# Small layernorm steps moved from VectorE to GpSimd, with new orders on all engines, in a four-layer graph network on one core

## The reference

```
h = relu(layernorm(x));  x = x + deg*(h Wi + b) + adj (h Wj)                    # layer 0
h = relu(layernorm(x));  x = x + softmax(mask(leaky(src_i + dst_j))) (h W)      # layer 1, 0 for a row without neighbours
h = relu(layernorm(x));  x = x + [softmax(mask(leaky(src_i + dst_j))) g | g], g = h W   # layer 2
h = relu(layernorm(x));  x = x + multi-head attention(h), 8 heads of 32, masked # layer 3
layernorm(x) = (x - mean) / sqrt(variance + 1e-5)
```

## Time and profile before

| | |
|---|---|
| median of 3 runs | 1277.61 us |
| the profiled execution's own time | 1276.93 us |
| its span | 1275.1 us |
| TensorE busy | 1232.8 us (97%) |
| TensorE weight loads busy | 1134.8 us (89%) |
| VectorE busy | 1141.8 us (90%) |
| ScalarE busy | 1058.2 us (83%) |
| GpSimd busy | 944.5 us (74%) |
| granted TensorE clock, mean | 0.995 |

### The profile page before, as it was taken

How to read it: one execution, slowest core, us unless ns; L and a number is a source line. 1 busy time by engine, 2 the same in 40 slices (tenths; PEclk the granted TensorE clock), 3 DMA queues, 4 the chain that set the end, 5 groups by cost and what they waited for, 6 DMA issues and landing times. The chain is left out here.

```text
span 1275.1 us, 43341 instructions
## 1 busy us (share of the span) xinstructions
PE 1232.8 (97%) x12213; PEld 1134.8 (89%) x12213; DVE 1141.8 (90%) x5713; ACT 1058.2 (83%) x3911; POOL 944.5 (74%) x1338
## 2 busy tenths in 40 slices
PE   5799999999999999999999999999999999999997
PEld 4689999999999999999999998999999999999986
DVE  4689999989999999999999999999999999998874
ACT  2468898888888888888889888888889888888886
POOL 4568877877777877777787787777787777787663
PEclk9899999999999999999999999999999999999999
DMA  4011222222112122222112122222122122211001
GB/s 119 24 22 21 38 44 50 37 44 51 36 44 52 36 44 52 36 43 52 38 40 52 40 45 46 41 39 52 40 47 43 41 46 44 43 39 31 18 19 34
DMA packets 70586, 53.57 MB, mean 42 GB/s; under 512 B 20688, under 2 KB 70352, under 8 KB 70352
## 3 DMA queue, kind: packets, MB, share of 16 engines
q1 hardware_dynamic: 68144, 49.35, 19.2%
q10 hardware_dynamic: 2208, 1.45, 0.4%
HBM read 33.89 MB, written 16.89 MB: 40 GB/s over the span
## 5 line engine op out<-in xcount | busy, mean ns | idle before, releaser
L775 ACT ACTIVATE exps<-masked,nmax 128x128 f32<-128x128 f32 x1024 | 397.1, 394 | 0.0
L348 POOL TENSOR_TENSOR probs<-exps,rsum 128x512 f32<-128x512 f32 x256 | 266.7, 1042 | 162.6 <-DVE rsum L567 161.9
L319 POOL TENSOR_SCALAR y<-x,nm,rstd 128x256 f32<-128x256 f32 x512 | 282.8, 563 | 22.5 <-issue 21.0
L311 POOL TENSOR_TENSOR rstd<-veps,power 128x2 f32<-128x2 f32 x256 | 178.2, 696 | 114.4 <-DVE veps L472 109.3
L559 DVE CUSTOM_DVE_ANT_0 masked<-bank,mask 128x128 f32<-128x128 f32 x1024 | 232.0, 280 | 1.3 <-PE bank L986 0.8
L775 ACT ACTIVATION_READ_ACCUMULATOR exps<-masked,nmax 128x1 f32 x1024 | 198.4, 194 | 0.0
L876 PE MATMUL bank<-w_hi,ht_hi 128*128 128x512 f32 (+1 forms) x512 | 192.6, 376 | 4.5 <-DVE ht_lo L501 4.5
L456 DVE BATCH_NORM_STATS2 stats<-x 128x6 f32<-128x256 f32 x512 | 183.9, 411 | 0.2
L886 PE MATMUL bank<-ident,y 128*128 128x128 f32 x1024 | 159.0, 278 | 20.0 <-POOL y L319 19.3
L877 PE MATMUL bank<-w_lo,ht_hi 128*128 128x512 f32 (+1 forms) x512 | 175.4, 343 | 0.0
L878 PE MATMUL bank<-w_hi,ht_lo 128*128 128x512 f32 (+1 forms) x512 | 174.8, 341 | 0.0
(11 more groups left out here) (120 smaller groups left out, 3693.4 us busy)
## 6 DMA issues: line engine op xcount, KB each, us to landing
x<-in_x SPq DMA_DIRECT2D x64, 256.0 KB, 4.6
out<-x SPq DMA_DIRECT2D x64, 256.0 KB, 4.7
db<-rows SPq DMA_DIRECT2D x110, 128.0 KB, 4.1
rows<-dst SPq DMA_DIRECT2D x110, 1.0 KB, 3.0
probs<-in_w0t SPq DMA_DIRECT2D x1, 512.0 KB, 7.9
probs<-in_w1t ACTq DMA_DIRECT2D x1, 256.0 KB, 5.9
exps<-in_wot SPq DMA_DIRECT2D x1, 256.0 KB, 7.6
w_sb<-in_w ACTq DMA_DIRECT2D x1, 256.0 KB, 7.8
```

What stands on the lines that cost most here:

```text
L311: pool.tensor_tensor(rstd[i][:, b], veps[i][:, b], power[:], ALU.pow).then_inc(S[f"rstd{i}"], 1)
L319: last = pool.tensor_scalar(y[i][:, b, g], src[:, bx, g], nm[i][:, s, g:g + 1], rstd[i][:, s, g:g + 1], ALU.add, ALU.mult)
L348: pool.tensor_tensor(probs3[:, p % BUFFERS["probs3"], j], exps3[:, p % BUFFERS["exps3"], j], rsum3[:, s, j].unsqueeze(2).to_broadcast([P, ...
L775: last = act.activation(exps3[:, b, j, i], masked3[:, p % BUFFERS["masked3"], j, i], ACT.Exp, bias=nmax3[:, s, j, i:i + 1], scale=-1.0, ac ...
```

## The change

The eps addition and the negated mean of all four layernorms, and layer 1's product with the row flag, go from VectorE to GpSimd. `negative_mean` becomes an operation of its own with the names `nm0` to `nm3` and its own place in the list. `rstd` and `y` keep their instructions. `LAG`, `BANKS` and the order in every `step`, SyncE's too, are new; `BUFFERS` and `SMALL` are as before.

```diff
@@ GpSimd gains
+            def shifted_variance(i, p):
+                b = p % SMALL
+                passed(pool, f"mv{i}", p)
+                passed(pool, f"rstd{i}", p, SMALL)
+                pool.tensor_scalar(veps[i][:, b], mv[i][:, b, :, 1], LN_EPS, None, ALU.add).then_inc(S[f"veps{i}"], 1)
+
+            def negative_mean(i, reader, p):
+                b = p % SMALL
+                passed(pool, f"mv{i}", p)
+                passed(pool, reader, p, SMALL)
+                pool.tensor_scalar(nm[i][:, b], mv[i][:, b, :, 0], -1.0, None, ALU.mult).then_inc(S[f"nm{i}"], 1)
+
+            def clear_empty_rows(p):
+                s = p % SMALL
+                passed(pool, "rsum1_any", p)
+                pool.tensor_tensor(rsum[1][:, s], rsum[1][:, s], has_any[:].to_broadcast([P, G]), ALU.mult).then_inc(S["rsum1"], 1)
@@ VectorE loses
-            def shifted_variance(i, p):
-                b = p % SMALL
-                passed(dve, f"mv{i}", p)
-                passed(dve, f"y{i}", p, SMALL)
-                dve.tensor_scalar(veps[i][:, b], mv[i][:, b, :, 1], LN_EPS, None, ALU.add).then_inc(S[f"veps{i}"], 1)
-                dve.tensor_scalar(nm[i][:, b], mv[i][:, b, :, 0], -1.0, None, ALU.mult).then_inc(S[f"nm{i}"], 1)
-            def clear_empty_rows(p):
-                s = p % SMALL
-                passed(dve, "rsum1_any", p)
-                dve.tensor_tensor(rsum[1][:, s], rsum[1][:, s], has_any[:].to_broadcast([P, G]), ALU.mult).then_inc(S["rsum1"], 1)
@@ LAG, one line of 16 on either side
-       "row_in1": 0, "load": -4, "row_out2": 1, "store": 7, "row_out1": -1, "row_in2": 1, "e1t": 2, "h0t": -1, "pt0": 6, "wh0_mm": 1, "v_mm": 5,
+       "store": 8, "row_out1": 0, "row_in1": 0, "row_out2": 1, "load": -5, "row_in2": 1, "x2_mm": 2, "pt1": 6, "s0": 0, "wh0_mm": 1, "m1": -1,
```

More of the change, by code:

```diff
@@ L59 @@
[L59 to L72, removed]
@@ L73 @@
-    "x3b": (0, "x3_mm", ('x3',)),
-    "wh1": (2, "wh1_mm", ('wh1',)),
-    "hh": (1, "hh_mm", ('hh',)),
+    "x2b": (4, "x2_mm", ('x2',)),
+    "pt1": (2, "pt1", ('p3t_1',)),
+    "x1b": (5, "s0", ('x1',)),
+    "wh0": (0, "wh0_mm", ('wh0',)),
+    "m1": (4, "m1", ('mj_lo1', 't0_1')),
+    "h3t": (6, "h3t", ('h3t_lo',)),
+    "pt0": (3, "pt0", ('p3t_0',)),
+    "d2": (2, "d2", ('z2',)),
+    "pt3": (0, "pt3", ('p3t_3',)),
+    "x4b": (1, "x4_mm", ('x4',)),
+    "prep": (2, "products", ('w1_split',)),
@@ new lines @@
+    "m0": (5, "m0", ('mj_lo0', 't0_0')),
+    "qt": (6, "qt_mm", ('qt',)),
+    "h2t": (3, "h2t", ('ht2',)),
+    "at2": (2, "e2t", ('at2',)),
+    "kt": (4, "kt_mm", ('kt',)),
+    "d1": (3, "d1", ('z1',)),
+    "x3b": (1, "x3_mm", ('x3',)),
+    "h1t": (0, "h1t", ('h1t_lo',)),
+    "ot": (6, "ot_mm", ('ot_lo',)),
+    "sc0": (2, "scores", ('nmax3_0',)),
+    "sc1": (3, "scores", ('nmax3_1',)),
+    "sc2": (4, "scores", ('nmax3_2',)),
+    "sc3": (5, "scores", ('nmax3_3',)),
+    "hh": (1, "hh_mm", ('hh',)),
@@ L76 @@
+    "v": (0, "v_mm", ('v',)),
+    "h0t": (3, "h0t", ('h0t_lo',)),
+    "pt2": (1, "pt2", ('p3t_2',)),
+    "at1": (2, "e1t", ('at1',)),
+    "wh1": (6, "wh1_mm", ('wh1',)),
+    "prepa": (0, "adj_spread", ('adj_rows',)),
+    "zz1": (7, "z1", ('nmax1',)),
     "zz2": (7, "z2", ('nmax2',)),
[L77 removed]
 }
@@ L186, in gnn_kernel @@
         x_out = [sem(f"x_out{i}") for i in range(BUFFERS["x4"])]
-        S = {name: sem(name) for name in LAG if name not in ("row_in1", "load", "row_out2", "store", "row_out1", "row_in2")}
-        for name in ("nm0", "nm1", "nm2", "nm3",):
-            S[name] = sem(name)
+        S = {name: sem(name) for name in LAG if name not in ("store", "row_out1", "row_in1", "row_out2", "load", "row_in2")}
         def due(t, operation):
@@ L270, in step @@
                     write_row(1, t - LAG["row_out1"])
+                if due(t, "row_in1") and not at_an_end(t - LAG["row_in1"]):
+                    spread_row(1, t - LAG["row_in1"])
+                if due(t, "row_out2") and not at_an_end(t - LAG["row_out2"]):
+                    write_row(2, t - LAG["row_out2"])
+                if due(t, "load") and t - LAG["load"] >= 2:
+                    load(t - LAG["load"])
                 if due(t, "row_in2") and not at_an_end(t - LAG["row_in2"]):
@@ L585, in step @@
             def step(t):
+                if due(t, "stats0"):
+                    stats_of(0, x0, t - LAG["stats0"])
+                if due(t, "x4"):
+                    sum_x4(t - LAG["x4"])
                 if due(t, "rsum3_0"):
                     inverse_sum3(0, t - LAG["rsum3_0"])
+                if t == LAG["w0_low"]:
+                    low_w0()
+                if due(t, "qt"):
+                    add_bias("qt", qt, bq_sb, float(DH) ** -0.5, t - LAG["qt"])
+                if t == LAG["w1_split"]:
+                    split_w1()
@@ L588, in step @@
                 if due(t, "rsum2"):
                     inverse_sum(2, "rsum2", "x3", t - LAG["rsum2"])
+                if due(t, "mj_lo0"):
+                    low_mj(0, t - LAG["mj_lo0"])
+                if due(t, "t0_0"):
+                    add_own(0, t - LAG["t0_0"])
+                if due(t, "mv0"):
+                    mean_and_variance(0, t - LAG["mv0"])
+                if due(t, "kt"):
+                    add_bias("kt", kt, bk_sb, 1.0, t - LAG["kt"])
+                if due(t, "x3"):
+                    sum_x3(t - LAG["x3"])
@@ new lines, in step @@
+                if due(t, "exp3_1"):
+                    exps3_of(1, t - LAG["exp3_1"])
+                if due(t, "at1"):
+                    copy_exp_transposed(1, t - LAG["at1"])
+                if due(t, "h0t_hi"):
+                    relu_transposed_high(0, ht0_r, last_of("m0", "m1"), t - LAG["h0t_hi"])
+                if due(t, "v"):
+                    copy_v(t - LAG["v"])
+                if due(t, "wh1"):
+                    copy_projection1(1, t - LAG["wh1"])
+                if due(t, "p3t_2"):
+                    copy_p3_transposed(2, t - LAG["p3t_2"])
@@ new lines, in step @@
+                if due(t, "h3t_hi"):
+                    relu_transposed_high(3, ht3_r, last_of("kt_mm", "qt_mm", "v_mm"), t - LAG["h3t_hi"])
+                if due(t, "p3t_0"):
+                    copy_p3_transposed(0, t - LAG["p3t_0"])
+                if due(t, "z2"):
+                    sum_logits(2, hh, "hh", F1, t - LAG["z2"])
+                if due(t, "exp3_0"):
+                    exps3_of(0, t - LAG["exp3_0"])
+                if t == LAG["w3_high"]:
+                    round_w3()
```

313 lines of the change are left out of this document (130 added, 183 removed), and 21 rows, old and new, of the table LAG.

## The result

| | before | changed |
|---|---|---|
| median beside each other | 1277.3 us (1275.94 to 1278.38, 4 runs) | 1265.3 us (1264.62 to 1268.02, 4 runs) |
| span of the profiled execution | 1275.1 us | 1263.1 us |

That holds on this chip.

What follows compares the result with a forecast made beforehand. TensorE, busy 97%, was taken as the bound, with an 18.88 us pass. Disturbed passes -3.2, start +0.7 and the other ends +0.6 gave -1.9 us: median 1277.6 to 1275.7 us, own range 1272 to 1279, whole range 1267 to 1286.

Steps and rivals of the forecast that it cites:

- net of the filling and draining without the start: +0.6: Both ends besides the start: longer hops and new list places net to +0.6 us, bounds -8 and +6.
- signs of being wrong: Filling: among them, s0 (an aggregation's first matmul) of pass 8 starting more than 5 us away from 141.7.
- Filling, the hops: Layernorm chains: a hop to GpSimd adds +0.25 us to five y waits and one in the draining, +1.5.
- Filling, the lists: Filling, new order: scores behind kt_mm -1.2 us; layernorm 2 ahead of layernorm 1 on GpSimd -1.3 and +1.6.
- Draining: End of the run: ScalarE's work and the last pass's tail stay the same, 0 beyond one longer y chain.
- Start: First pass: r0 precedes the first veps on GpSimd, first transpose at 13.2 us, +0.7, bounds 0 and +1.3.
- GpSimd's cover: Steady pass: GpSimd needs 17.3 us of 18.88 with the added work, 1.6 us to spare, so no cost.
- Rival C: GpSimd becomes the bound: small instructions at 696 ns, pass 21.9 us, 1446 us in all; chance 0.03.
- VectorE: Steady pass: VectorE loses 2.18 us of 17.64, 15.46 remain; directly worth nothing.
- Disturbed passes: Steady part: half of the 6.5 us lost in disturbed passes goes, -3.2 us, bounds -6.5 and +8.
- rival B: Layernorm 1: mv1 behind nmax2 lets late rows reach y1 and h1t; 1292 us, or 1286; chance 0.15.
- Rival A: Ends: qt waits go, -2.4 us, filling's y waits halve, -3; with disturbed passes 1269.5 us; chance 0.17.

Runs made afterwards that it cites:

- e1_move: Kernel before with only the small instructions moved to GpSimd, lists and banks as before: 1302.63 us, ratio 1.0145.
- e7_thrice: Changed kernel with two more instructions of veps's form ahead of each veps on GpSimd, into an unread tile: 1281.64 us, ratio 1.0045.
- e9_h1: Changed kernel with h1t_hi ahead of z1 on ScalarE and h1t_lo ahead of nmax1 and stats3 on VectorE: 1272.48 us, ratio 0.9980.
- e2_lists: Changed kernel with the small instructions back on VectorE, lists and banks as changed: 1330.65 us, ratio 1.036.
- e3_warm_before: Kernel before with 8 extra transposes in TensorE's waits for y of layernorms 1 and 2, passes 0 to 3: 1283.63 us, ratio 1.0003.
- c_before: Kernel before, unchanged, run on chip 3 for its trace: profiled execution 1279.02 us.
- c3_after: Changed kernel, unchanged, run on chip 5: 1265.74 us, ratio 0.9919 to the kernel before.

## Why the prediction was wrong

Wrong, and by the step "net of the filling and draining without the start: +0.6". It measured -7.1 and -3.5. One of the signs of being wrong that I had named came true: s0 of pass 8 starts at 134.66, 7.0 us away from 141.7. The two ends got shorter, which the traces of the changed kernel show on five chips; through which places of the new lists is shown only in part.

- *Filling, the hops.* I counted +0.25 us on five chains. The hop itself was nearly right. Where GpSimd stands idle for mv, 0.59 us pass from mv's end to rstd's start (0.60 in `e1_move`), against 0.28 before: +0.31. (The 0.71 at the start, 9.20 to 9.91, has the last 0.12 us of r0 in it.) What was wrong is how often it counts. `e1_move` pays 5 to 6 us, as much as 17 to 19 such hops, and its waits for y grow from 6.1 to 12.1 us. `e7_thrice` takes the 0.59 to 0.93 and pays 6.8 us, as much as 20 times the difference. Between the first s0 and that of pass 8, 27 such chains begin. TensorE's list of waits names only the last link of a chain that runs through several layernorms; I priced the five waits as if they were independent. How much of it is chains in series and how much is queueing on GpSimd was not followed.
- *Filling, the lists.* If `e1_move`'s 5 to 6 us are in the changed kernel too, the new lists give back about 12 to 13. I had a -1.2 and a -1.3 for two of their places. That a pair of places can be worth this much is shown by `e9_h1` (5.4 us), but that pair is no part of the change: z1 stands ahead of h1t_hi and nmax1 ahead of h1t_lo in the kernel before as well. So the split of the 12 to 13 over the new places stays open, and by `e2_lists` (122.9) they are worth nothing with the small instructions on VectorE. Of TensorE's waits in the filling, those for y, ht_lo, qt and mj_lo made 12.3 us; all waits make 9.3 now. I had read the earlier trace rows as if they were all for y or qt, and left out the 3.3 us for ht_lo, which fell to 1.0. The rest is TensorE's own rows: three stretches at half clock fewer, 3.4 us each, which by `e3_warm_before` are hardly worth anything by pass 8, and 11 matmuls that now come after it, about 1.1 us at 1044.94 / 10457, and are paid in the draining.
- *Draining.* Forecast 0, found -3.5, in two traces that have no half clock there. The lists carry most of it: `e2_lists`, at full clock too, has 86.2 where the kernel before has 88.5. The moved instructions carry nothing that can be seen: `e1_move` has 89.7 and `c_before` 89.9, each with one stretch of 3.4 us at half clock. TensorE waited 14 times, 8.5 us, and now 7 times, 5.9 us. I took the last pass's tail for the whole; the seven passes ahead of it run by the lists too. Which places do it is open.
- *Start.* +0.7 forecast: the first transpose moved from 12.46 to 13.03 (+0.6), but s0 only by 0.1.
- *Undisturbed pass.* 18.88 forecast, 18.86 found: right.
- *GpSimd's cover.* 17.3 us a pass forecast, 1.6 to spare: that it is covered was right, the size was not. In the steady part of `c3_after` GpSimd waits 69 us for other engines, so that it needs (1042.3 - 69) / 55 = 17.7 us a pass, and 1.2 are to spare. Small instructions took 0.22 instead of 0.19, and there are more gaps between its instructions than I had counted. `e7_thrice` keeps it busy 1.3 us a pass longer, a little more than it has to spare; GpSimd then waits 6 us for others in all, and the pass is 19.06. The flag product took 0.195 us there, not the 0.31 that I had worked out. Rival C falls.
- *VectorE.* 15.46 us forecast, 16.55 found. The rows of small instructions overlap with each other and with their neighbours (two starts 0.08 us apart at a length of 0.17), so their mean lengths may not be summed: of the 17.64 us a pass the rows that were to go covered only 1.23 by themselves. It changed nothing in the time.
- *Disturbed passes.* -3.2 forecast. On chip 1 the steady part became 1.5 us shorter, on chip 3 it is 15 us longer than that of the kernel before. What I called rival B was half right: late rows do reach TensorE, but not through mv1, y1 and h1t. No trace has a steady wait of TensorE for y. In the two places that I followed they come through a bank (h1t_lo, v_mm) and through x4 and kt. I had asked only which data a late instruction delivers, not which bank it frees.
- *Rival A* (the ends shorter, 1269.5) had the right side and, with qt and y, two of the three waits that shrank, and half the size.

| chip | before | changed | ratio |
|---|---|---|---|
| 1 | 1277.3 | 1265.3 | 0.9916 |
| 3 | 1280.92 | 1282.48 | 1.0026 |
| 4 | 1274.1 | 1265.85 | 0.9939 |
| 5 | 1275.87 | 1265.74 | 0.9919 |
| 6 | 1286.58 | 1302.67 | 1.0119 |

(On chip 2 the changed kernel did not run.) The change trades a fixed gain of some 10 us at the ends for a steady part that follows late landings more: 12 us won on a prompt chip, 16 lost on the slowest.

## What to carry to other kernels

In the filling of a pipeline an addition to a chain that every layer repeats can count far more often than the table shows waits for it (here 17 to 20 times, against 5 waits); measure its price by lengthening the chain. When orders are redrawn, follow not only data but banks and buffers: an instruction behind a DMA's wait is late for everyone whose bank it frees. And a kernel whose passes hang on small DMAs should be measured on several chips before a gain of one per cent is believed; here a third buffer for the stored tile and two instructions moved out from behind the row's wait, in the middle passes only, had the lowest median of the three kernels on both chips where they ran, by 18.7 us against the changed kernel on the late chip and by about 2 us of their own on the prompt one. And compare the ends of two traces only where the granted clock is the same in both.

## What the runs showed of the hardware

- One program's time differs between chips: the changed kernel from 1265.3 to 1302.67 us. On chip 3, 16.9 us of it go with ScalarE's wait for the row. The medians of the landings are hardly apart (the spread row 3.7 and 3.9 us on chips 1 and 6, the stores 5.3 and 6.0), and the changed kernel's fillings agree within 1.5 us. The tail differs, above all that of the 1 KB write which the spread row waits for: of its 110 transfers 1 took over 6 us from issue to landing on chip 1, 6 on chip 3 and 13 on chip 6. ScalarE waited 24 times for a row on chip 1 and 80 times on chip 6.
- A tensor_scalar on two elements a partition takes 0.22 us on GpSimd (228 and 220 ns), against 0.17 us on VectorE undisturbed and 1.02 to 1.25 us when a long GpSimd instruction runs beside it.
- In the filling, stretches of 3.4 us at half clock (1.2 GHz) cost the kernel before next to nothing: 119.4 us without them, 119.8 with three and 120.4 with four. In the draining they show: the changed kernel takes 85.0 us there without one (chips 1, 3 and 6), 86.2 with one (chip 4) and 87.7 with 6.8 us of half clock (chip 5).
